# Attention weights prepared one block further ahead, and propagation layers with the adjacency block as the stationary operand

## The reference

```python
cur = x; acc = x
for _ in range(3):
    msgs = edge_weight[:, None] * cur[dst]
    cur = segment_sum(msgs, src, 3125)     # cur = A @ cur
    acc = acc + cur
x = layernorm(x + acc)

h = x @ W_node.T                            # 4 heads of 32
e = edge_attr @ W_edge.T
att = leaky_relu(sum([h[src], h[dst], e] * a))        # per edge and head
m = max(segment_max(att, dst), 0)
ex = exp(att - m[dst])
w = ex / (segment_sum(ex, dst) + (E - deg) * exp(-m))[dst]
h_prime = segment_sum(w * h[src], dst)
x = layernorm(x + h_prime)
```

## Time and profile before

| | us |
|---|---|
| median of 3 runs (lowest to highest) | 1869.33 (1863.49 to 1871.24) |
| the profiled execution | 1875.85 |
| its span, first to last instruction | 1874.1 |
| busy in it: TensorE / weight loads / VectorE / ScalarE | 1410.6 / 1099.2 / 1008.1 / 611.2 |
| layers, first to last matmul of line 614 | 622.9 to 1036.2 |
| attention pipeline, first weight copy to last product | 1269.2 to 1849.6 |

### The profile page before, as it was taken

One profiled execution on the slowest core, in us unless ns is written; L12 is line 12 of the kernel. 1 busy time (PEld: TensorE's weight loads), 2 busy tenths in 40 slices (PEclk: granted clock), 3 DMA queues, 4 the chain that ended last, 5 costly groups with the idle time before them and its releaser, 6 DMA issues.

```text
span 1874.1 us, 63741 instructions
## 1 busy us (share of the span) xinstructions
PE 1410.6 (75%) x28181; PEld 1099.2 (59%) x28182; DVE 1008.1 (54%) x1574; ACT 611.2 (33%) x1526; POOL 103.5 (6%) x123
## 2 busy tenths in 40 slices
PE   3399999755544799999999488865777777777774
PEld 2399999644443344444444388864555665656663
DVE  8812222498886000200200589977777777777784
ACT  0022222344443000000000400006676676666674
POOL 0051200000000000000000000010000000000000
PEclk9999655677777899999999789997888888888887
DMA  6032422177777986486585065530000000000001
GB/s 194 1 114 98 148 93 93 32 175 173 173 173 177 355 304 239 175 307 219 186 307 208 22 225 205 202 108 19 15 15 15 15 15 15 15 15 15 15 3 36
DMA packets 129741, 230.11 MB, mean 123 GB/s; under 512 B 22984, under 2 KB 109543, under 8 KB 121222
## 3 DMA queue, kind: packets, MB, share of 16 engines
q1 hardware_dynamic: 116614, 215.11, 35.2%
q0 software_dynamic: 4000, 8.20, 1.6%
q10 hardware_dynamic: 8928, 3.72, 0.8%
HBM read 179.08 MB, written 47.91 MB: 121 GB/s over the span
## 4 chain that ended last, share of the span: by engine, by line
PE 51%; DVE 14%; SPq 12%; issue 7%; ACT 7%; DVEq 7%; DMA 1%; ACTq 0%; POOL 0%; POOLq 0%
PE bank L614 22%; SPq L284 11%; PE bank L725 8%; PE bank L532 8%; PE bank L711 5%; PE bank L523 5%; ACT pt L914 4%; DVE z_sb L1309 4%; DVE oh_lo L1009 3%; DVE qhw L1363 3%; DVEq L1362 2%; DVE osT L1296 2%; DVEq L1298 2%; ACT wt L904 1%; DVEq L1321 1%
## 5 line engine op out<-in xcount | busy, mean ns | idle before, releaser
L614 PE MATMUL bank<-ablk,cur 128*128 128x512 f32 (+1 forms) x1050 | 405.8, 550 | 23.9 <-DMA ablk<-adj 21.9
L914 ACT COPY pt<-bank 128x400 f32<-128x400 f32 x800 | 329.5, 525 | 144.2 <-PE bank L711 144.1
L711 PE MATMUL bank<-qhw,qh_s 64*128 64x104 f16 x6400 | 230.2, 226 | 162.0 <-ACT pt L914 88.7
L614 PEld LDWEIGHTS bank<-ablk,cur 128*128 128x128 f32 x1050 | 189.2, 191 | 240.7 <-issue 238.2
L711 PEld LDWEIGHTS bank<-qhw,qh_s 64*128 64x128 f16 x6400 | 180.5, 105 | 212.1 <-ACT pt L914 134.4
L1139 DVE COPY curT<-bank 128x512 f32<-128x512 f32 (+1 forms) x21 | 13.0, 633 | 416.8 <-PE bank L614 416.7
L593 PE MATMUL bank<-oh_s,ohw 64*26 64x128 bf16 x9600 | 126.5, 280 | 115.8 <-ACT at L831 95.7
L1363 DVE TENSOR_TENSOR qhw<-qhb,wt 128x3328 f16<-128x3328 f16 x100 | 189.3, 1893 | 7.8 <-issue 0.4
L593 PEld LDWEIGHTS bank<-oh_s,ohw 64*26 64x26 bf16 x9600 | 113.5, 110 | 129.3 <-issue 126.0
L725 PE MATMUL bank<-pt,hx 128*32 128x128 f32 x5000 | 181.5, 308 | 0.8 <-ACT pt L914 0.8
L532 PEld LDWEIGHTS bank<-wedge,eaT 128*128 128x128 f32 (+1 forms) x832 | 177.5, 314 | 1.4
(11 more groups left out here) (164 smaller groups left out, 1243.9 us busy)
## 6 DMA issues: line engine op xcount, KB each, us to landing
ablk<-adj SPq DMA_DIRECT2D x65, 1600.0 KB, 7.7
adj<-at SPq DMA_DIRECT2D x200, 208.0 KB
srow<-row_d SPq DMA_DIRECT2D x26, 992.0 KB, 4.9
ea<-in_edge_attr SPq DMA_DIRECT2D x25, 992.0 KB, 6.8
brow<-row_d SPq DMA_DIRECT2D x26, 248.0 KB, 5.5
ee_d<-eet ACTq DMA_DIRECT2D x13, 124.0 KB, 2.6
z_d<-z_sb ACTq DMA_DIRECT2D x26, 62.0 KB, 3.1
out<-cur SPq DMA_DIRECT2D x2, 768.0 KB
```

The source lines that it names most:

```text
L614: m = pe.matmul(bank[g][:, 0:w], cur[:, b, :], ablk[:, u, g * BANK:g * BANK + w], start=(n == 0 and u == 0), stop=(n == NR - 1 and u == RI ...
L711: m = pe.matmul(bank[(g % 2) * 2 + hf][:, v * (H * B1):(v + 1) * (H * B1)], qh_s[r, q % 2, t, :], qhw[r, q % 2, t, k * H:(k + 1) * H, :].r ...
L914: m = act.copy(pt[:, par, :, :, d0:d0 + 4], bank[(g % 2) * 2 + hf][:, 0:4 * H * B1] .rearrange("p (v h b) -> p h b v", v=4, h=H)[:, :, 0:N ...
```

## The change

In the layers the adjacency block becomes the stationary operand and the features the moving one, 25 matmuls of 128 columns for each block row j, where there were 7 of up to 512. The banks then hold the new features untransposed. The copies to `curT`, the turning back and their semaphores (`lay_sb`, `lay_T`) go. Features alternate between `cur` and the memory of `curT` (`stack(l)`); ScalarE copies banks 0 to 6 there after layers 0 and 1, VectorE adds from there, and after the last layer straight from the banks. Since four blocks now share a bank, each bank is first cleared by a bfloat16 matmul of zeros. Only the loads of block row j's own features and of the bank in question are waited for at the start of a layer.

In the attention `scores` and `exps` of block j+2 stand at the end of step j; VectorE's `split_weights(j+1)` comes after quarter 0, TensorE's `turn_weights(j+1)` after quarter 1, ScalarE's `weights(j+1)` after `quarter_out` 1.

```diff
+        def stack(l):
+
+            return cur if l % 2 == 0 else curT[:, :].rearrange("p (b n) -> p b n", b=NB)
...
                 pe.wait_ge(s["at_sb"], NB * 2 * AB + AB)
+                pe.wait_ge(s["ld_x"], 64)
                 for l in range(LAYERS):
-                    if l == 0:
-                        pe.wait_ge(s["ld_x"], 64)
-                    else:
-                        pe.wait_ge(s["cur_sb"], l * len(groups))
+                    source = stack(l)
                     for n, rg in enumerate(row_groups(l)):
                         for u in range(RING):
-                            b = rg * RING + u
+                            j = rg * RING + u
                             pe.wait_ge(s[f"a{u}"], 16 * (l * (NR - 1) + n + 1))
+                            if l and n == 0 and u == 0:
+                                pe.wait_ge(s["cur_sb"], (l - 1) * len(groups) + j // BPB + 1)
                             for g, bs in enumerate(groups):
-                                w = len(bs) * P
-                                m = pe.matmul(bank[g][:, 0:w], cur[:, b, :], ablk[:, u, g * BANK:g * BANK + w],
-                                              start=(n == 0 and u == 0), stop=(n == NR - 1 and u == RING - 1))
+                                if l and n == 0:
+                                    if u == 0:
+                                        pe.wait_ge(s["cur_sb"], (l - 1) * len(groups) + max(g, j // BPB) + 1)
+                                    elif g == 0:
+                                        pe.wait_ge(s["cur_sb"], l * len(groups))
+                                if n == 0 and u == 0:
+                                    pe.matmul(bank[g][:, 0:len(bs) * P], identb[:, :], zerob[:, 0:len(bs) * P], start=True, stop=False)
+                                for k, b in enumerate(bs):
+                                    m = pe.matmul(bank[g][:, k * P:(k + 1) * P], ablk[:, u, b * P:(b + 1) * P],
+                                                  source[:, j, :], start=False, stop=(n == NR - 1 and u == RING - 1 and k == len(bs) - 1))
...
-                    for g, bs in enumerate(groups):
-                        pe.wait_ge(s["lay_sb"], l * len(groups) + (g + 1))
-                        for k, b in enumerate(bs):
-                            m = pe.transpose(bank[g][:, k * P:(k + 1) * P], curT[:, b * P:(b + 1) * P], ident[:, :])
-                        m.then_inc(s["lay_T"], 1)
...
             def step(j, par, head=False, end=False):
                 for q in range(NQ):
-                    if q == NQ - 1 and not end:
+                    quarter(j, q)
+                    if q == 1 and not end:
                         turn_weights(j + 1)
-                    quarter(j, q)
...
-                for l in range(LAYERS):
-                    if l:
-                        act.wait_ge(s["acc_sb"], l * NB)
+                for l in range(LAYERS - 1):
                     for g, bs in enumerate(groups):
-                        act.wait_ge(s["lay_T"], l * len(groups) + (g + 1))
-                        act.copy(cur[:, bs[0]:bs[0] + len(bs), :].rearrange("p b n -> p (b n)"),
+                        act.wait_ge(s["lay_ps"], l * len(groups) + (g + 1))
+                        if l:
+                            act.wait_ge(s["acc_sb"], (l - 1) * len(groups) + (g + 1))
+                        act.copy(stack(l + 1)[:, bs[0]:bs[0] + len(bs), :].rearrange("p b n -> p (b n)"),
...
-            def step(j, par, head=False, end=False):
+            def step(j, par, head=False, ahead=2):
                 quarter_out(j, 0, par)
-                if not end:
-                    exps(j + 1)
                 quarter_out(j, 1, par)
+                if ahead > 0:
+                    weights(j + 1, 1 - par)
                 quarter_out(j, 2, par)
-                if not end:
-                    weights(j + 1, 1 - par)
                 if not head:
                     feature_out(j - 1, 1 - par)
                 quarter_out(j, 3, par)
+                if ahead > 1:
+                    exps(j + 2)
...
-            def step(j, par, n, head=False, end=False):
+            def step(j, par, n, head=False, ahead=2):
                 quarter(j, 0, par)
-                if not end:
-                    scores(j + 1, 1 - par, n)
+                if ahead > 0:
+                    split_weights(j + 1)
                 quarter(j, 1, par)
-                quarter(j, 2, par)
                 if not head:
                     finish(j - 2, par)
-                if not end:
-                    split_weights(j + 1)
+                quarter(j, 2, par)
                 quarter(j, 3, par)
+                if ahead > 1:
+                    scores(j + 2, par, n)
```

More of the change, by code:

```diff
@@ L210, in build @@
             oh_ready at_ps at_sb at_full at_armed adj_out0 adj_out1
-            a0 a1 a2 a3 a4 a_used0 a_used1 a_used2 a_used3 a_used4 lay_ps lay_sb lay_T cur_sb acc_sb
+            a0 a1 a2 a3 a4 a_used0 a_used1 a_used2 a_used3 a_used4 lay_ps cur_sb acc_sb
             x1_ready x1T_ps x1T_sb h_ps h_sb al_ready
@@ L938, in fast_attention @@
                 weights(0, 0)
+                exps(1)
                 step(0, 0, head=True)
@@ L942, in fast_attention @@
                     step(i * 2 + 2, 0)
-                step(NB - 2, 1)
-                step(NB - 1, 0, end=True)
+                step(NB - 2, 1, ahead=1)
+                step(NB - 1, 0, ahead=0)
                 feature_out(NB - 1, 0)
@@ L1137, in fast_layers @@
                     for g, bs in enumerate(groups):
-                        dve.wait_ge(s["lay_ps"], l * len(groups) + (g + 1))
-                        dve.tensor_copy(curT[:, g * BANK:g * BANK + len(bs) * P], bank[g][:, 0:len(bs) * P])\
-                            .then_inc(s["lay_sb"], 1)
-                    for b in range(NB):
-                        if b % BPB == 0:
-                            dve.wait_ge(s["cur_sb"], l * len(groups) + (b // BPB + 1))
-                        dve.scalar_tensor_tensor(out=acc[:, b, :], in0=xs[:, b, :] if l == 0 else acc[:, b, :],
-                                                 scalar=2.0 if l == 0 else 1.0, in1=cur[:, b, :],
-                                                 op0=ALU.mult, op1=ALU.add,
-                                                 **(dict(accum_out=st[:, 0, b:b + 1]) if l == LAYERS - 1 else {}))\
-                            .then_inc(s["acc_sb"], 1)
+                        if l < LAYERS - 1:
+                            dve.wait_ge(s["cur_sb"], l * len(groups) + (g + 1))
+                        else:
+                            dve.wait_ge(s["lay_ps"], l * len(groups) + (g + 1))
+                        for k, b in enumerate(bs):
+                            made = stack(l + 1)[:, b, :] if l < LAYERS - 1 else bank[g][:, k * P:(k + 1) * P]
+                            m = dve.scalar_tensor_tensor(out=acc[:, b, :], in0=xs[:, b, :] if l == 0 else acc[:, b, :],
+                                                         scalar=2.0 if l == 0 else 1.0, in1=made,
+                                                         op0=ALU.mult, op1=ALU.add,
+                                                         **(dict(accum_out=st[:, 0, b:b + 1]) if l == LAYERS - 1 else {}))
+                        m.then_inc(s["acc_sb"], 1)
                     dve.drain()
@@ L1401, in fast_attention @@
                 split_weights(0)
-                step(0, 0, 0, head=True)
+                scores(1, 1, 0)
+                step(0, 0, 1, head=True)
                 step(1, 1, 1, head=True)
-                with dve.Fori(0, NB // 2 - 1) as i:
-                    step(i * 2 + 2, 0, i + 1)
+                with dve.Fori(0, NB // 2 - 2) as i:
+                    step(i * 2 + 2, 0, i + 2)
                     step(i * 2 + 3, 1, i + 2)
-                step(NB - 1, 0, 0, end=True)
+                step(NB - 3, 0, NB // 2)
+                step(NB - 2, 1, 0, ahead=1)
+                step(NB - 1, 0, 0, ahead=0)
                 finish(NB - 2, 1)
```

## The result

The changed kernel takes 1840.47 us, median of 4 runs (1836.90 to 1845.11); the kernel before beside it 1866.41, median of 4 (1857.93 to 1871.24). The ratio is 0.986, 95% interval 0.983 to 0.989. The same two kernels in a later comparison, with thirteen runs of the old one and four of the new, gave 0.982 (0.978 to 0.986). So the change makes it 1.4 to 1.8% faster, 26 to 32 us. The forecast was 1862, its range 1836 to 1884.

A forecast was written before the change was run, and what follows sets the result against it. TensorE's pace was taken to bound the layers, the round trip between engines the attention. Layers +7 and attention -14 gave -7 from the median 1869.33, hence 1862 us, range 1836 to 1884.

The forecast's parts named there:

- Layers, +7 forecast: Three layers: slower weight-load and matmul pairs +14.4, clearing +4.5, shorter gaps -11.9; sum +7 us, bounds -9 and +22.
- The clearing: Layers: zeroing the banks by bfloat16 matmuls, uncovered on TensorE, 1.5 us a layer, 4.5 in all.
- The gaps: After layers 0, 1, 2: 3.7 becomes 0.7, 3.8 becomes 0.1, 6.5 becomes 1.3 us; 11.9 saved.
- in series: Layers: rival that weight load and matmul run one after the other, 0.219 us a pair, +416 in all; chance 0.01.
- the loop through `exps`: Attention: from one end of `exps` to the next, through split, quarters and product, 20.6 us a block against 21.54.
- the back edge late by 3.1: Attention: at the hardware loop's jump back, TensorE's product ends 8.3 us after `exps`, making that block 3.1 late.
- the other arm: Attention: after `exps`, VectorE's split 1.6 and quarter 1 until TensorE starts 3.6, together 5.2 us.
- The other block: Attention: the block of each pair away from the hardware loop's back edge, taken as 0.6 us late.
- The gathers priced at nothing: Attention: GpSimd's gathers still run two blocks ahead of their use and cost nothing.
- the rival in which the back edge hides wholly: Attention: pause covered by `exps`, clock stays up, pair 41.2 to 43.3 us; at 42.5, total 1832; chance 0.15.
- Layers with dearer loads: Layers: rival that weight loads meet a busy DMA, 0.12 to 0.125 us a pair, total 1894 to 1913; chance 0.07.
- an attention without gain: Attention: rival that another of the mixed engines takes over at once; +7, total 1876 us; chance 0.08.

The follow-up runs named there:

- chip B: Chip of the second batch of follow-up runs; the unchanged kernel before took 1872.0 us there, the changed kernel 1840.1, ratio 0.982.
- chip A: Chip of the first batch of follow-up runs, a slower one; the kernel before took 1916.6 us there.
- half_exps: Changed kernel with the exponentials of only two of four heads from block 2 on, so no longer computing the attention; 1832.2 us, ratio 0.978 to the kernel before.
- after_body4: Changed kernel with four blocks instead of two in the body of TensorE's hardware loop; 1832.9 us, ratio 0.978 to the kernel before.
- chip C: Chip of the third batch of follow-up runs, a slower one; the kernel before took 1915.4 us there.

## Why the prediction was right, and where it was not

The total is right by its sign and its range (1836 to 1884), but the range held by 4 us only: 1840 lies 22 below the forecast of 1862 and outside the 1847 to 1871 that the forecast had as its own. The change is worth 26 us, on chip B 32, where 7 were forecast. The direction followed from the mechanism; that the range held owes something to its width.

- **Layers, +7 forecast, +6.1 measured (+5.2 on chip B, +5.9 on chip A).** The pace taken was 0.1115 a pair; the trace has 0.111 to 0.112. Without the clearing TensorE takes 139.65 us for 1250 pairs in a layer, 0.1117. The clearing was put at 4.5 and is 3.1: a full bank takes 0.22 and layers 1 and 2 cost 1.4 each, as forecast, while layer 0 shows 0.3. The gaps are closed as walked: 0.76 for 0.7, none for 0.1, sums complete 0.95 us behind TensorE for 1.3. One reading was off, with little effect: 62.76 / 350 is 0.18 and not 0.19, which makes the pace of bare loads 0.113 and not 0.111. The lower bound of the layers should read -10 for -9. The rule of the Trainium skill ("TensorE: Matmul & The Clock Gate", Part 3), by which load and MATMUL with the same rows don't overlap, is contradicted by 1250 pairs with all 128 rows in 140.6 us, 0.1125 a pair with the clearing in it, where bare loads alone pace at 0.111 to 0.113; in series it would be 0.219. A sentence of its Part 2 has loads into the background buffer of weights pulled ahead of matmuls in flight; the overlap in the trace agrees with it, but which buffer a load went to no trace shows.
- **Attention, the loop through `exps`, 20.6 forecast.** The shortest blocks take 20.71, and half_exps, in which they shorten by 0.8, shows that it is this loop. The wait for line 899 (now 905), forecast at 1 us a block, is 1.5. The wait for line 904 (now 910) is gone. Right.
- **Attention, the back edge late by 3.1: the step that failed.** It is late by 22.20 - 20.71 = 1.5. Of the 8.3 from the end of `exps` to the end of the product, 0.6 became 1.23, 4.55 became 3.45, and 3.1 became 2.57 (the granted clock is 0.83 in that product, for 0.69 before): 7.2. The largest part, 1.1, is the second pause in quarter 0, which I took over from the earlier trace rows as if it belonged to the back edge. It doesn't: it is in all six profiles with the old layers and in none of the eight with the new ones, whichever the attention's order, always behind the 38th matmul, and it ends 1.2 to 1.6 us after a packet of instructions has landed. It is TensorE waiting for its instructions at one place of the program. The new layers change TensorE's program ahead of the loop, and that this moves the place out of quarter 0 is the likely reason; that was not tried by itself. Against the 5.2 of the other arm this walk still leaves the block 2.0 late, where the mean is 1.5: of the miss of 1.6 it explains 1.1. The other block was put late by 0.6 and is by 0.5. Together (3.1 - 1.5 + 0.1 - 2 x 0.1) x 12, 18 us, the 0.1 being what the loop takes more than forecast. The attention's stage gains 34 to 36 for 14; the rest lies in the first two blocks, 6.1 shorter, for which the forecast had nothing in sum.
- **The gathers priced at nothing.** In the first comparison and on B true. On A and C they go with 1.3 us a block, and there the attention alone gains only 7 us by the medians, where the changed kernel gains 34 to 36 in this stage on the others. I had asked when the gathers land, and not whom they disturb while they are issued.
- **The rivals.** The pair of 43.34 lies just above the 41.2 to 43.3 of the rival in which the back edge hides wholly; it doesn't hide wholly, since some 1.0 us of it remains (after_body4). Layers with dearer loads, in series, and an attention without gain are all excluded in the first comparison.

## What to carry to other kernels

What a loop's back edge costs changed here with code that stands ahead of the loop: take it from the profile as a range, not as a fixed term, look among the DMA packets whether a pause for "issue" ends behind a packet of instructions, and look for what work of another engine already covers it before unrolling. The same edit was worth 1.0 us an edge in one kernel and 3.0 in another. A wait on the critical engine can often be removed by moving the small handover (here the weight copy) earlier, at the price of computing its input one step further ahead; when such a step moves, ask of every DMA it issues or releases beside whose work it will now fall. And test each half on the same chip as the whole: here the layers' code takes a pause out of the attention's loop, and chips differ by more than the change is worth.

## What the runs showed of the hardware that was not expected

- The same kernel takes 1866 to 1872 us in two comparisons and 1915 to 1917 in two others, in 4 to 26 runs each. In all eight profiles of the slower chips TensorE and ScalarE stand still for 10 us and more beside a run of 24 gathers of GpSimd, in none of the six others.
- On the slower chips, two pauses of 0.3 us fall into TensorE's product just behind the ends of two indirect gathers of GpSimd, in all six kernels whose gathers end there, and stretch 64 matmuls from 1.89 to 3.2 us.
- Both pauses of TensorE at a loop's back edge, 3.0 to 3.6 us and 0.5 to 1.5, end 1.2 to 1.9 us after a 16 KB packet of instructions has landed. The second stands behind the same 38th matmul each time, and is there or not with code that ran hundreds of microseconds earlier.
- Of a back edge of 3.3 us of idle TensorE, some 1.0 is seen in the time on chip B, where another engine's step lies beside it; on chip C, with the second pause and the same order, 3.0.
- One matmul that starts an accumulation is enough for a bank into which four matmuls write 128 columns each; the clearing by zero matmuls cost 3.1 us here. It was not run together with the loop over four blocks.
